# Four chained graph layers on one core: the input read a second time, and the second basis mixed by quarter matrices from the first unit on

## What is computed

```python
x = _layernorm(x + L0(x))   # h = GCN(x); h = gelu(batch_norm(h)); return h + x
x = _layernorm(x + L1(x))   # two SAGE layers: relu(h @ Ws + mean_neighbours(h) @ Wn + b)
x = _layernorm(x + L2(x))   # two gated relational layers over 2 edge types
x = _layernorm(x + L3(x))   # relu((h + sum_neighbours(h)) @ W1 + b1) @ W2 + b2
```

## Time and profile before

| | us |
|---|---|
| median of 3 runs | 958.25 |
| runs, lowest to highest | 957.13 to 961.15 |
| the profiled execution | 959.76 |
| its span | 957.8 |
| busy in it: PE | 899.9 (94%) |
| busy: DVE | 684.1 (71%) |
| busy: ACT | 280.2 (29%) |
| busy: POOL | 85.5 (9%) |

### The profile page before, as it was taken

How to read it: one execution, slowest core, us unless ns; L and a number is a source line. 1 busy time by engine, 2 the same in 40 slices (tenths; PEclk the granted TensorE clock), 3 DMA queues, 4 the chain that set the end, 5 groups by cost and what they waited for, 6 DMA issues and landing times.

```text
span 957.8 us, 13083 instructions
## 1 busy us (share of the span) xinstructions
PE 899.9 (94%) x4320; PEld 434.2 (45%) x4320; DVE 684.1 (71%) x1469; ACT 280.2 (29%) x431; POOL 85.5 (9%) x66
## 2 busy tenths in 40 slices
PE   6799999998996999988799799999999999999996
PEld 2354555554554544433344344444444444444442
DVE  6598898854437879798899999999834244442358
ACT  0132345443873313424031211111711131132220
POOL 1000011120111002103021000000600010010000
PEclk9899999999997999999799999999999999999998
DMA  8755565558112495788644675664041014322236
GB/s 285 233 176 155 156 179 163 158 142 186 44 45 67 109 241 167 193 249 160 178 125 128 136 186 157 181 159 116 1 99 34 1 49 115 90 66 44 44 88 195
DMA packets 133371, 126.97 MB, mean 133 GB/s; under 512 B 80417, under 2 KB 80886, under 8 KB 133306
## 3 DMA queue, kind: packets, MB, share of 16 engines
q10 hardware_dynamic: 94784, 57.69, 24.5%
q1 hardware_dynamic: 38522, 68.45, 24.3%
HBM read 95.24 MB, written 12.52 MB: 113 GB/s over the span
## 4 chain that ended last, share of the span: by engine, by line
PE 65%; DVE 19%; DMA 6%; issue 3%; ACT 3%; DVEq 1%; POOL 1%; ACTq 1%; SPq 1%
PE Dp L669 23%; PE Dp L639 22%; PE T L595 9%; PE Dp L551 5%; PE Dp L694 5%; DVE acc L1205 4%; DMA stage<-in_basis 2%; DVE stt L1297 2%; DVE Zraw L1316 1%; DMA wst<-mixd 1%; DVE w L1334 1%; DVE Zraw L1274 1%; DVE S L1282 1%; POOL Zraw L508 1%; DMA Zraw<-in_basis 1%
## 5 line engine op out<-in xcount | busy, mean ns | idle before, releaser
L639 PE MATMUL Dp<-W,hT 128*128 128x512 f16 x816 | 182.9, 383 | 6.6 <-DMA hT<-S 3.2
L669 PE MATMUL Dp<-Zraw,A 128*128 128x512 f16 x800 | 173.0, 379 | 0.0
L1205 DVE SCALAR_TENSOR_TENSOR acc<-stage,att,acc 128x512 f32<-128x512 f32 x232 | 166.6, 788 | 4.0 <-DMA stage<-in_basis 4.0
L669 PE MATMUL Dp<-Zraw,AT 128*128 128x512 f16 x600 | 130.0, 379 | 0.0
L639 PEld LDWEIGHTS Dp<-W,hT 128*128 128x128 f16 x816 | 80.1, 99 | 103.6 <-issue 8.4
L669 PEld LDWEIGHTS Dp<-Zraw,A 128*128 128x128 f16 x800 | 78.3, 98 | 94.4
L1098 DVE TENSOR_SCALAR Zraw<-hT,w 128x640 f16<-128x640 f16 (+1 forms) x240 | 111.1, 463 | 0.1
L669 PEld LDWEIGHTS Dp<-Zraw,AT 128*128 128x128 f16 x600 | 58.7, 98 | 70.8
L1096 DVE TENSOR_SCALAR Zraw<-hT,w 128x128 f16<-128x128 f16 (+1 forms) x240 | 66.7, 278 | 27.0 <-PE Dp L551 18.1
L551 PE MATMUL Dp<-Zraw 128*128 128x320 f16 (+1 forms) x480 | 74.7, 302 | 1.6 <-DVE Zraw L1098 1.0
L922 ACT ACTIVATE Zraw<-Dp,zsc 128x512 f16<-128x512 f32 x50 | 32.2, 684 | 133.7 <-PE Dp L639 131.1
(11 more groups left out here) (169 smaller groups left out, 905.2 us busy)
## 6 DMA issues: line engine op xcount, KB each, us to landing
stage<-in_basis SPq DMA_DIRECT2D x180, 256.0 KB, 2.9
Zraw<-in_basis SPq DMA_DIRECT2D x60, 256.0 KB, 2.9
xres<-w ACTq DMA_DIRECT2D x30, 256.0 KB, 2.3
xr<-xres ACTq DMA_DIRECT2D x30, 256.0 KB, 2.9
wst<-in_Wn ACTq DMA_DIRECT2D x4, 1024.0 KB, 5.7
wst<-in_Ws ACTq DMA_DIRECT2D x4, 1024.0 KB, 5.6
wst<-mixd ACTq DMA_DIRECT2D x4, 1024.0 KB, 5.9
wst<-in_root ACTq DMA_DIRECT2D x3, 1024.0 KB, 5.7
```

The source lines that it names most:

```text
L639: last = nc.tensor.matmul(Dp[:, j, m, :], turned[:, hp, k * P:(k + 1) * P], weights_of(u, m)[:, wp, k, :], start=(n == 0), stop=(n == 3 * ...
L669: last = nc.tensor.matmul(sum_bank(t), a[:, k, ds(t * P, P)], Z[:, r, h, k, :], start=(n == 0), stop=(n == count - 1))
L1205: last = v.scalar_tensor_tensor(part, stage[:, q, :], a, part, ALU.mult, ALU.add)
```

## The change

Five things are changed together.

1. The input is loaded a second time. ScalarE issues ten loads (`load_input`): the first two at the start of unit 0's aggregation, the others behind `deviation` of the tile two before. They go into `xr`, and `join_input` reads `xr` there, and waits for the load.
2. So `acc` is free once `split_x` has read the input, and the basis products may start in unit 0. They wait for that once (`x_hi`).
3. The list counts quarters (two instructions) and no longer halves (four). The total, 120 quarters, is the same.
4. Unit 0 has six turned places: two more (`mida`, `midb`) in a part of `Zraw` that held basis matrices during the counting. `turn_to` runs six tiles ahead at the start and in `z_out`.
5. The three semaphores of the edge loads become one.

```diff
-        HALVES = {
-            ("dense", 1): [0, 0, 0, 0, 1, 1, 1, 1, 1, 1],
-            ("agg", 1): [1, 1, 1, 1, 0, 1, 0, 1, 0, 1],
-            ("dense", 2): [1, 1, 1, 1, 1, 2, 1, 1, 2, 1],
-            ("dense", 3): [2] * NT,
-            ("agg", 3): [3, 3, 3, 3, 3, 0, 0, 0, 0, 0],
+        QUARTERS = {
+            ("dense", 0): [0, 0, 1, 0, 1, 1, 1, 0, 1, 1],
+            ("agg", 0): [6, 4, 4, 3, 0],
+            ("dense", 1): [0, 0, 0, 0, 2, 2, 2, 2, 2, 2],
+            ("agg", 1): [2, 2, 1, 1, 1, 2, 1, 2, 1, 1],
+            ("dense", 2): [1, 1, 2, 2, 2, 2, 2, 2, 2, 2],
+            ("dense", 3): [3, 4, 3, 4, 3, 4, 3, 4, 3, 4],
+            ("agg", 3): [4, 4, 4, 4, 2, 0, 0, 0, 0, 0],
         }
...
+        mid = Zraw[:, 3 * NT * D:3 * NT * D + 4 * D]
...
-        HT_RING = {0: ["w1a", "w1b", "a", "b"], 2: ["a", "b", "fara", "farb"], 3: ["a", "b", "wsta", "wstb"],
+        HT_RING = {0: ["w1a", "w1b", "mida", "midb", "a", "b"], 2: ["a", "b", "fara", "farb"], 3: ["a", "b", "wsta", "wstb"],
...
-            sp.dma_start(dst_i, dst_t).then_inc(e_dst, 16)
-            sp.dma_start(typ_i, typ_t).then_inc(e_typ, 16)
-            sp.dma_start(src_i, src_t).then_inc(e_src, 16)
+            sp.dma_start(dst_i, dst_t).then_inc(e_edge, 16)
+            sp.dma_start(typ_i, typ_t).then_inc(e_edge, 16)
+            sp.dma_start(src_i, src_t).then_inc(e_edge, 16)
...
+                    elif slot[:3] == "mid" and t < 4:
+                        act.wait_ge(s_mx, PAIRS * GROUPS)
...
+            def load_input(t):
+
+                if t > 1:
+                    act.wait_ge(s_v, t - 1)
+                else:
+                    act.wait_ge(x_hi, NT)
+                rows = min(P, N - t * P)
+                act.dma_start(xr[0:rows, t % 2, :], x[t * P:t * P + rows, :]).then_inc(e_again[t % 2], 16)
...
-                        turn_to(t + 4, u)
+                        turn_to(t + (4 if u else 6), u)
...
-                    turn_to(4, 0)
+                    turn_to(6, 0)
...
+                    for t in range(2):
+                        load_input(t)
                     for t in range(NT // 2):
                         out_degree(t)
...
                         deviation(t, t % 2)
+                        if t < NT - 2:
+                            load_input(t + 2)
...
-            def mix_halves(count):
+            def mix_quarters(count):
 
                 for n in range(mixed[0], mixed[0] + count):
-                    b, h = n // 2, n % 2
+                    b, q = n // KT, n % KT
                     if n == 0:
                         dve.wait_ge(s_att, 16)
-                    for q in (2 * h, 2 * h + 1):
...
+                        dve.wait_ge(x_hi, NT)
+                    dve.wait_ge(st_full[q], 16 * (b + 1))
+                    for r in range(REL):
...
                     dve.wait_ge(s_tb, t + 1)
-                    v.scalar_tensor_tensor(w2[:, j, :], x_in(t), 2.0, Dp[:, j, 2, :], ALU.mult, ALU.add).then_inc(s_v, 1)
+                    dve.wait_ge(e_again[j], 16 * (t // 2 + 1))
+                    v.scalar_tensor_tensor(w2[:, j, :], xr[:, j, :], 2.0, Dp[:, j, 2, :], ALU.mult, ALU.add).then_inc(s_v, 1)
...
                     dve.wait_ge(s_bn, 48)
+                    weight_work("agg", 0, 0)
                     for b in range(KT):
                         block_stats(b)
+                        weight_work("agg", 0, b + 1)
```

More of the change, by code:

```diff
@@ L200, in resnorm_gnn_kernel @@
         LN = [u for u in range(NU) if UNITS[u]["ln"]]
-        e_src, e_dst, e_typ, e_row, e_x = (sem(n) for n in ("e_src", "e_dst", "e_typ", "e_row", "e_x"))
+        e_edge, e_row, e_x = (sem(n) for n in ("e_edge", "e_row", "e_x"))
         s_pad = sem("s_pad")
@@ L242, in resnorm_gnn_kernel @@
         s_wlo = sem("s_wlo")
-        s_hT = {n: sem(f"s_hT_{n}") for n in ("a", "b", "w1a", "w1b", "fara", "farb", "wsta", "wstb", "stga", "stgb")}
+        s_hT = {n: sem(f"s_hT_{n}") for n in ("a", "b", "w1a", "w1b", "mida", "midb", "fara", "farb", "wsta", "wstb", "stga", "stgb")}
         s_d = sem("s_d")
@@ L267, in resnorm_gnn_kernel @@
         x_sc, x_hi = sem("x_sc"), sem("x_hi")
+        e_again = [sem(f"e_again{j}") for j in range(2)]
         ds = bass.ds
@@ L370, in loaded @@
             return 16 * at[-1 if last else 0]
-        HALVES = {
-            ("dense", 1): [0, 0, 0, 0, 1, 1, 1, 1, 1, 1],
-            ("agg", 1): [1, 1, 1, 1, 0, 1, 0, 1, 0, 1],
-            ("dense", 2): [1, 1, 1, 1, 1, 2, 1, 1, 2, 1],
-            ("dense", 3): [2] * NT,
-            ("agg", 3): [3, 3, 3, 3, 3, 0, 0, 0, 0, 0],
+        QUARTERS = {
[6 more added lines that the diff above has]
+            ("agg", 3): [4, 4, 4, 4, 2, 0, 0, 0, 0, 0],
         }
-        assert sum(sum(n) for n in HALVES.values()) == 2 * BASES
+        assert sum(sum(n) for n in QUARTERS.values()) == KT * BASES
         SUM_BANK = [(0, 2), (1, 2), (0, 0), (0, 1), (1, 0), (1, 1), (0, 2), (1, 0), (1, 1), (1, 2)]
@@ L1062, in _ @@
                                 ALU.mult).then_inc(s_mixT, 1)
-            dve.wait_ge(e_typ, 16)
-            dve.wait_ge(e_dst, 16)
-            dve.wait_ge(e_src, 16)
+            dve.wait_ge(e_edge, 48)
             link(v.tensor_copy(src_f, src_i))
@@ L1189, in _ @@
             mixed = [0]
-            def mix_halves(count):
+            def mix_quarters(count):
                 for n in range(mixed[0], mixed[0] + count):
-                    b, h = n // 2, n % 2
+                    b, q = n // KT, n % KT
                     if n == 0:
                         dve.wait_ge(s_att, 16)
-                    for q in (2 * h, 2 * h + 1):
-                        dve.wait_ge(st_full[q], 16 * (b + 1))
-                        for r in range(REL):
-                            part = acc[:, r, q, :]
-                            a = att[:, r, b:b + 1]
-                            if b == 0:
-                                last = v.tensor_scalar(part, stage[:, q, :], a, None, ALU.mult)
-                            else:
-                                last = v.scalar_tensor_tensor(part, stage[:, q, :], a, part, ALU.mult, ALU.add)
-                        last.then_inc(st_free[q], 1)
+                        dve.wait_ge(x_hi, NT)
+                    dve.wait_ge(st_full[q], 16 * (b + 1))
+                    for r in range(REL):
+                        part = acc[:, r, q, :]
+                        a = att[:, r, b:b + 1]
+                        if b == 0:
+                            last = v.tensor_scalar(part, stage[:, q, :], a, None, ALU.mult)
+                        else:
+                            last = v.scalar_tensor_tensor(part, stage[:, q, :], a, part, ALU.mult, ALU.add)
+                    last.then_inc(st_free[q], 1)
                 mixed[0] += count
             def weight_work(kind, u, t):
-                mix_halves(HALVES.get((kind, u), [0] * NT)[t])
+                mix_quarters(QUARTERS.get((kind, u), [0] * NT)[t])
                 for step, *what in SCALES.get((kind, u, t), []):
```

4 lines of the change are left out of this document (2 added, 2 removed).

## The result

| | before | changed | ratio |
|---|---|---|---|
| median of 20 runs, us | 959.38 | 955.54 | 0.996 (0.9942 to 0.9978) |
| lowest to highest | 957.13 to 963.07 | 949.44 to 963.34 | |
| profiled execution | 959.76 | 955.46 | |
| its span | 957.8 | 953.5 | |

Faster by 3.8 us (0.4%), where 9.5 us were forecast: the direction is right, the size 2.5 times too large, and what was measured is inside what I had called no change.

The account below looks back on a forecast made before the run. VectorE was taken to bound dense 2, PE dense 3 to aggregation 4. Dense 2 starts 3.0 + 1.0 + 0.5 = 4.5 us later, yet aggregation 2's first sum comes 9.5 earlier: span 957.8 - 9.5 = 948.3, median 948.7, range 944.5 to 957.

Parts of the forecast that it names:

- what I had called no change: Whole kernel: a measurement tells about 0.5% (4.8 us) from no change; faster means below 953.5; chance of between 0.2.
- What bounds where: PE alone bounds dense 3 to aggregation 4, so products removed there give nothing; VectorE bounds 404 to 538 us.
- Six turned places: Start of unit 0: two more transposes ahead of ScalarE's square root delay PE's tile 2 by 3.0 us (up to 6.9).
- nothing is gained for it: Unit 0's dense stage: the two added places bring no gain, since PE waited for no turned tile in later tiles.
- Unit 0's products: Unit 0: six quarters in dense 0 cost nothing; those in its aggregation make it 1.0 us late (0 to 2).
- the last block: End of unit 0's aggregation: VectorE takes it late by 0.7 us, taken as 1.0 (0 to 2), delaying all behind.
- The second reading: Ten 256 KB input loads on ScalarE's queue: join 2 and unit 1's transposes together 0.5 us late, up to 1.5.
- Dense 2: VectorE needs 3.9 us a tile against PE's 5.18, so PE becomes the bound; ends at 466.5 us against 474.3.
- the forecast's own sum: First sum of aggregation 2 at 470.8 us in place of 480.28, 9.5 us earlier, with 1 us for `stage`.
- The check by VectorE alone: Dense 2: -8.0 - 1.3 - 2.45 + 4.5 = -7.3, and some 2 us of waits and stretched products: -9.3.
- my first rival: VectorE stays the bound in dense 2, so only the counted work goes: -4.8 us, 953.4; chance 0.18.
- whatever 480.28 moves by, the end moves by: From aggregation 2's first sum (480.28 us): VectorE's layernorm and gates set the pace to 538, so the shift passes unchanged.

Follow-up runs that it names:

- e1: Changed kernel with four turned places in unit 0 instead of six, second reading and quarter list kept: 952.13 us, ratio 0.9912 to the kernel before.
- e3: Changed kernel with its six places, but the square root of the degrees ahead of the two added transposes: 951.15 us, ratio 0.9905 to the kernel before.
- e2: Changed kernel with the old list of products in quarters, none in unit 0 and 24 in dense 2: 963.33 us, ratio 1.0029 to the kernel before.
- e9: Kernel before with only the second reading of the input added (four places, old list in quarters): 959.53 us, ratio 0.9992.
- e7: Changed kernel with GpSimd's low halves of unit 3's first two matrices and the second 1 MB load in dense 2 both cut to 16 columns: 953.56 us.
- e4: Changed kernel with 7 quarters in dense 2 (not 18), 40 in dense 3 (not 35), 24 in aggregation 3 (not 18): 951.32 us.
- e8: Changed kernel with the square root ahead of the two added transposes and 7 quarters in dense 2, 40 in dense 3, 24 in aggregation 3: 948.12 us.
- e10: e8 with ScalarE issuing unit 1's first transpose ahead of the fourth load of the input, not behind it: 947.36 us, ratio 0.9868 to the kernel before.
- e11: e10 with 5, 4, 3, 3 quarters in unit 0's aggregation, 3 in dense 2 (not 7), 30 in aggregation 3 (not 24): 947.55 us, ratio 0.9869.
- e5: Changed kernel with GpSimd's low halves of unit 3's first two matrices computed on 16 of 512 columns: 952.08 us, ratio 0.9919 to the kernel before.

## Why the prediction was right in its parts and wrong in its sum

*What bounds where*: right. Behind the 72 products of the restart in dense 3 every kernel takes 402.3 to 402.6 us, whatever dense 3 and aggregation 3 held in products. The restart itself took 16.98 to 18.65 us, which the forecast did not have.

*Six turned places*: +3.0 forecast, 2.55 measured at the third tile; the two issues took 2.75 us together, 1.38 each. The lower bound of 1.51 us for an issue was too high: both kernels have transposes that are issued in 1.25 us. The Trainium skill (Advanced Engine Details and Errata, X-Bar Transpose (TRN2)) says that transposing DMAs are as fast as regular ones; carried over to the issue this gave 0.8 us for the two, and the issues here do not bear that out. The page does not speak of the issue. What was wrong is the other half, "nothing is gained for it". With the products' loads in dense 0, four places cost 2.1 us of waiting (e1), so the places are needed and their order at the start is the mistake (e3). I had weighed them against the trace of before, in which those loads were not there. I had also left out that a longer idle brings PE back at the lower clock for longer: 4.95 us for the first 12 products and not 4.24, with a granted clock of 0.50 and not 0.68 in the first 3 us.

*Unit 0's products*: cost nothing in dense 0, and the last block was taken 0.6 us late (1.0 forecast, from PE's idle of 2.19 and 1.58 us). Right; e2 shows that all of it is small.

*The second reading*: +0.5 forecast. The step that was too small is the transpose behind the fourth load: it landed in 4.0 us instead of 3.1, and PE restarted at 4.82 us for 12 products instead of 4.15. So of the 5.2 us at dense 2, 2.55 are there at the third tile, 2.0 more at dense 1 and 0.7 behind that restart. e9 alone shows about as much for the reading: 0.5 us between the third tile and dense 1, and a restart that is 1.0 longer.

*Dense 2*: this is the step that failed. From its start to the first sum it was forecast 14.0 us shorter (75.1 to 61.1) and was 9.7 shorter (65.4). "Now, with 2 quarters a tile at most, VectorE needs 1.26 + 2.65 = 3.9 us a tile against PE's 5.18, so PE becomes the bound", with 1 us added for `stage`. The unit prices were right where nothing else runs. It left out the work of the stage that is not products (a maximum of 2.3 us at tile 0 and the scales of tile 1, which make PE's idles of 0.40 and 0.56 us) and, above all, 5.2 us by which GpSimd stretches VectorE's products, with a wait of 3.38 us for `stage` and not 1. The row of 3.29 us was in the earlier trace rows; I read it as a trait of the wait ahead of it, in place of looking what GpSimd did at that time. Either one taken away brings the first sum to 260.3 to 261.5, and both to 260.6, where the forecast's own sum has 260.1. So the 5.1 us between forecast and measurement at that point, all but 0.5, go when these two go. That e7 meets the forecast this closely is in part luck: it starts dense 2 1.4 us later than forecast, and makes up for it by needing none of the 1 us for `stage` and a shorter first pair. And the 4.3 us that dense 2 took too long are not the fixed price of the two: e1 and e3 keep both, with the same list, and lose 2.2 to 2.4 us less.

The check by VectorE alone, -9.3, counted 2.45 us for PE's late tile and some 2 us of waits and stretches as gone. They stayed: in the changed kernel VectorE waits 0.72, 0.62 and 1.19 us for high halves (L937), the wait for `stage` fell by 0.4 us only and the stretches by 0.9.

The measured case is my first rival, VectorE stays the bound (953.4). Its reason, the load and the transposes beside the products' loads, is half of it; GpSimd was in no rival.

*From the first sum to the end*: "whatever 480.28 moves by, the end moves by" was off by 1.3 us: aggregation 2 took 59.06 us to dense 3 and not 57.76. Some 0.6 is a new wait for PE's second sum (479.18), since VectorE now begins at once and PE has no lead; 0.7 is GpSimd's L521, which stretched another instruction by more (2.65 against 1.92 us). e4 to e8, e10 and e11 show 59.06 to 59.13; e1 and e3, where the wait for the second sum is 0.25 us, show 58.74 and 58.75.

In sum, in the profile: -0.76 (ahead of unit 0) + 5.24 (to dense 2) - 9.67 (dense 2) + 1.30 (aggregation 2) - 0.41 (from the restart in dense 3) = -4.3 us, where the forecast had 0 + 4.5 - 14.0 + 0 + 0 = -9.5.

What stays open: how the two effects in dense 2 are coupled. In e5 GpSimd is quiet but the 1 MB load is there, and yet the wait for `stage` is gone and the transposes land in 7.8 and 5.2 us. That the places of `stage` are released earlier against the load, or that the load itself comes 1.0 us earlier, would explain it; no run separates these. And why the times of the changed kernel spread over 14 us while those before spread over 6 is not explained; its shortest execution (949.44) had a mean granted clock of 0.985 and its longest (963.34) 0.975.

## What to carry to other kernels

Count work out of the stage in which its engine is the bound, and only there: 11 quarter matrices that the change had taken out of stages bound by PE were worth 6.3 us at the end of dense 2 when taken from that stage, and 4.2 us of the whole. Issues of DMAs on a computing engine are work of that engine: whatever stands behind them in its program, here a square root of 0.2 us on which PE waits, goes first. And before a stage is called bound by another engine after a change, sum all its instructions, stretched ones included, and look what runs beside each instruction that takes longer than its like.

The shortest kernels here are e10 and e11, which can't be told apart. e10 is the change, with the square root ahead of the added transposes, dense 2 relieved and the first transpose of unit 1 ahead of the load. Its time is 0.9868 of that before, against 0.996 for the change.

## What the runs showed of the hardware

A tensor operation of GpSimd over 128x1024 f32 (2.1 us each, in pairs) and a product of VectorE on two SBUF tensors delay each other. In dense 2, where GpSimd's pair was under way first, single products went from 0.74 to 2.6 us and the pair from 4.2 to 4.7. In unit 0's aggregation, where twelve products were under way, they kept their 0.74 us and the first of GpSimd's two took 4.95 us; the same pair takes 4.23 in the kernel before, which has no products there (timelines of VectorE and GpSimd, changed kernel):

```profile
253.39 8.04 DVE L1222 SCALAR_TENSOR_TENSOR acc<-stage,att,acc 128x512 f32<-128x512 f32 x12
```

```profile
258.48 7.05 POOL L512 TENSOR_TENSOR W<-wst,W 128x1024 f16<-128x1024 f32 x2 [11.80 <-ACT W L841]
```

An instruction with one SBUF tensor is not free of it: L1323 took 1.52 us beside GpSimd's pair at 487.94, and 0.55 elsewhere. Left at 16 columns (0.45 us for the two) GpSimd's pair stretches no product.

The same idle of PE, 4.9 to 5.0 us ahead of dense 3's third tile, was followed by 72 products that took 16.98 to 18.65 us, with a granted clock of 0.78 and 0.50 in the six us behind it in the shortest and the longest case.

A DMA transpose of one tile lands in 3.1 us with nothing ahead, in 12.7 to 14.3 us behind a 1 MB load and beside the products' loads, and in 4.1 and 3.9 us when that load is 32 KB. In the stretch of VectorE's wait (450 to 454 us) the DMA engines are marked as busiest, of the seven stretches read between 430 and 475 us, while they move least (busy us of PE, PEld, DVE, ACT, POOL, then clock, DMA share, GB/s; the changed kernel):

```profile
443.80:450.00 6.20, 5.37 (x26) 2.31 (x25) 6.20 (x10) 0.60 (x1) 0.00 (x0) 1.00 1.03 253
450.00:454.00 4.00, 4.00 (x20) 1.80 (x19) 0.62 (x2) 3.43 (x4) 0.00 (x0) 1.00 1.29 83
```
